# Chunked cross-attention with instance norm: the mask's negatives laid in the score banks by the scalar engine

## The reference

```python
qh, kh, vh = proj(ctx, W_in, b_in)            # (tokens, 256) @ (256, 768), 8 heads of 32
scores = einsum('bnqhd,bnkhd->bnhqk', qh, kh) / sqrt(32)     # inside each chunk of 64
scores = scores + where(mask > 0, 0.0, -1e9)                 # by key
out = einsum('bnhqk,bnkhd->bnqhd', softmax(scores), vh)
out = (out @ W_out.T + b_out) * mask + x
return (out - mean(out, tokens)) * rsqrt(var(out, tokens) + 1e-5)
```

## Time and profile before

| what | value |
|---|---|
| median of 3 runs | 2059.18 us (2058.57 to 2062.14) |
| the profiled execution's own time | 2053.5 us |
| its span, first to last instruction | 2051.7 us |
| mean granted clock of TensorE | 0.991 of full speed |
| busy: PE / DVE / ACT / POOL | 97% / 82% / 72% / 76% |

### The profile page before, as it was taken

How to read it: one execution, slowest core, us unless ns; L and a number is a source line. 1 busy time by engine, 2 the same in 40 slices (tenths; PEclk the granted TensorE clock), 3 DMA queues, 4 the chain that set the end, 5 groups by cost and what they waited for, 6 DMA issues and landing times.

```text
span 2051.7 us, 95454 instructions
## 1 busy us (share of the span) xinstructions
PE 1999.4 (97%) x42504; PEld 1633.8 (80%) x42504; DVE 1682.0 (82%) x2053; ACT 1487.3 (72%) x2177; POOL 1560.4 (76%) x1062
## 2 busy tenths in 40 slices
PE   6999999999999999999999999999999999999994
PEld 5888888888888888888888888888788887887883
DVE  4788888888888888888888888888888887888884
ACT  4677777777777777777777777777777777776774
POOL 4777777787777777777778787777777777877773
PEclk9999999999999999999999999999999999999996
DMA  4456666556656556656555665556665556655554
GB/s 155 116 151 175 171 180 182 166 155 176 180 170 171 173 165 177 182 172 169 161 168 172 188 180 161 158 172 177 172 176 168 161 171 173 179 164 154 163 152 129
DMA packets 242904, 342.81 MB, mean 167 GB/s; under 512 B 28992, under 2 KB 94784, under 8 KB 242496
## 3 DMA queue, kind: packets, MB, share of 16 engines
q1 hardware_dynamic: 242496, 336.71, 57.0%
HBM read 168.82 MB, written 67.11 MB: 115 GB/s over the span
## 4 chain that ended last, share of the span: by engine, by line
PE 96%; issue 1%; POOL 1%; ACT 1%; DVE 0%; DMA 0%; SPq 0%; POOLq 0%; ACTq 0%; DVEq 0%
PE proj_bank L291 37%; PE proj_bank L323 19%; PE proj_bank L345 18%; PE o_bank L392 10%; PE score_bank L368 9%; PE score_bank L361 3%; POOL y L554 0%; DMA ctx_raw<-ctx 0%; POOL ctx_lo L544 0%; ACT y L495 0%; POOL neg_rows L567 0%; ACT ctx_hi L427 0%; POOL prob L537 0%; POOL o_lo L576 0%; ACT q_f L466 0%
## 5 line engine op out<-in xcount | busy, mean ns | idle before, releaser
L537 POOL TENSOR_TENSOR prob<-prob,recip 128x1024 f32<-128x1024 f32 x256 | 487.8, 1905 | 329.4 <-DVE recip L627 327.2
L612 DVE TENSOR_REDUCE row_max<-score_bank 128x16 f32<-128x1024 f32 x256 | 313.4, 1224 | 298.9 <-PE score_bank L368 297.9
L435 ACT ACTIVATE prob<-prob 128x1024 f32<-128x1024 f32 x256 | 271.5, 1060 | 283.1 <-DVE prob L616 283.1
L544 POOL TENSOR_TENSOR ctx_lo<-ctx_raw,ctx_hi 128x512 fp32r<-128x512 f32 x256 | 331.0, 1293 | 48.8 <-ACT ctx_hi L427 48.5
L291 PE MATMUL proj_bank<-ctx_hi,w_hi 128*128 128x512 f32 x1024 | 349.0, 422 | 5.7 <-POOL ctx_lo L544 4.3
L554 POOL TENSOR_TENSOR y<-y,x_raw 128x512 f32<-128x512 f32 x256 | 325.4, 1293 | 4.6 <-DVE y L655 4.6
L616 DVE TENSOR_TENSOR prob<-score_bank,row_max 128x1024 f32<-128x1024 f32 x256 | 313.4, 1224 | 8.8
L291 PE MATMUL proj_bank<-ctx_hi,w_lo 128*128 128x512 f32 x1024 | 320.6, 394 | 0.0
L291 PE MATMUL proj_bank<-ctx_lo,w_hi 128*128 128x512 f32 x1024 | 318.0, 392 | 0.0
L635 DVE STREAM_TRANSPOSE squares<-prob 128x1024 f32<-128x1024 f32 x256 | 315.8, 1234 | 2.0 <-POOL prob L537 2.0
L623 DVE TENSOR_REDUCE sums<-prob 128x16 f32<-128x1024 f32 x256 | 304.7, 1190 | 1.2 <-ACT prob L435 1.1
(11 more groups left out here) (44 smaller groups left out, 3781.9 us busy)
## 6 DMA issues: line engine op xcount, KB each, us to landing
ctx_raw<-ctx SPq DMA_DIRECT2D x128, 512.0 KB, 5.8
x_raw<-x SPq DMA_DIRECT2D x128, 512.0 KB, 4.6
prob_t<-squares SPq DMA_DIRECT2D x1024, 64.0 KB, 2.5
out<-y SPq DMA_DIRECT2D x128, 512.0 KB, 6.0
mask_all<-mask SPq DMA_DIRECT2D x128, 256.0 KB, 4.2
v_x<-v_f SPq DMA_DIRECT2D x256, 128.0 KB, 3.5
y<-w_in_t SPq DMA_DIRECT2D x1, 768.0 KB, 4.4
y<-w_out_t SPq DMA_DIRECT2D x1, 256.0 KB, 4.4
```

The lines of the kernel that those rows point to most:

```text
L537: pool.tensor_tensor(part, part, slots(recip[:, u % 2, :]), ALU.mult).then_inc(norm_done, 1)
L544: pool.tensor_tensor(ctx_lo[:, n % 2, :, tokens], ctx_raw[:, n % BLOCKS, :, tokens], ctx_hi[:, n % 2, :, tokens].bitcast(F32), ALU.subtrac ...
L612: dve.tensor_reduce(row_max[:, :].rearrange("p (r c) -> p r c", c=CPU), rows, AX_X, ALU.max).then_inc(max_done, 1)
```

## The change

The eight mask matmuls of each unit go. In their place the scalar engine copies the negatives, now in fp32, into the four score banks (`lay_negatives`), a unit ahead, behind `high_attention`; the scores wait for that copy (`seeded`) and accumulate on it. Eight matmuls of zeros at the start (`open_banks`) put the banks in the state in which matmuls add. The copy of the attention output into `o_f` goes, and VectorE makes the low part of attention for both units, straight from `o_bank`. GpSimd loses its `low_attention` and gains the second half of the normalise, ahead of `divide`; the scalar engine keeps the first half.

```diff
@@ tensor, scores
-                wait(pe, less_done, count(B, UNITS, u))
-                for r in range(ROWS):
-                    masked = neg_rows[r * DH:r * DH + 1, j % 2, h * UNIT:(h + 1) * UNIT]
-                    for f in range(HALVES):
-                        pe.matmul(score_bank[f * CHUNK:(f + 1) * CHUNK, r, 0:UNIT], ones_row[r * DH:r * DH + 1, :],
-                                  masked, start=True, stop=False, skip_group_check=True)
+                pe.wait_ge(seeded, count(B, UNITS, u + 1))
...
+            def open_banks():
+                for r in range(ROWS):
+                    head = slice(r * DH, (r + 1) * DH)
+                    for f in range(HALVES):
+                        last = pe.matmul(score_bank[f * CHUNK:(f + 1) * CHUNK, r, 0:UNIT], zero_rows[head, 0:CHUNK],
+                                         zero_rows[head, :], start=True, stop=True, skip_group_check=True)
+                last.then_inc(opened, 1)
@@ tensor, probs_times_v
-                if h == 0:
-                    wait(pe, o_lo_done[1], n)
-                else:
-                    pe.wait_ge(o_f_done, n + 1)
+                wait(pe, o_lo_done, UPB * n + h)
@@ scalar
+            def lay_negatives(B, u):
+                if not unit_there(B, u):
+                    return
+                j, h = u // UPB, u % UPB
+                if h == 0:
+                    act.wait_ge(neg_done, count(B, BLOCKS, j + 1))
+                if B == 0 and u == 0:
+                    act.wait_ge(opened, 1)
+                wait(act, less_done, count(B, UNITS, u))
+                act.activation(score_bank[:, :, 0:UNIT], neg_rows[:, j % 2, h * UNIT:(h + 1) * UNIT].unsqueeze(
+                    1).broadcast_to([P, ROWS, UNIT]), ACT.Copy).then_inc(seeded, 1)
...
-                    normalise(done, 0)
+                    normalise(done)
...
                     high_attention(B, u - 2)
-                    if h == 0:
-                        copy_attention(B, u - 2)
-                    normalise(done, 1)
+                    lay_negatives(B, u + 2)
                     copy_squares(B, u)
@@ gpsimd
+            def normalise(n):
+                if not block_there(0, n):
+                    return
+                batch, j = n // BLOCKS, n % BLOCKS
+                if j == 0:
+                    pool.wait_ge(shift_done, batch + 1)
+                part = y[:, batch % 2, 1, j, :]
+                pool.tensor_scalar(part, part, rstd[:, 1:2], shift[:, 1:2], ALU.mult, ALU.add).then_inc(z_done[1], 1)
...
                         masked_keys(B, j + 1)
-                        low_attention(B, u - 2)
                     else:
...
+                    normalise(BLOCKS * (B - 1) + u - 5 if u >= 5 else BLOCKS * (B - 2) + 3 if u == 0 else -1)
                     divide(B, u + 1)
@@ vector
-                dve.tensor_tensor(o_lo[:, m % 2, 1, :, :], o_units, o_hi[:, m % 2, 1, :, :].bitcast(F32),
-                                  ALU.subtract).then_inc(o_lo_done[1], 1)
+                dve.tensor_tensor(o_lo[:, m % 2, h, :, :], o_units, o_hi[:, m % 2, h, :, :].bitcast(F32),
+                                  ALU.subtract).then_inc(o_lo_done, 1)
...
-                    if h == 1:
-                        low_attention(B, u - 2)
+                    low_attention(B, u - 2)
@@ buffers and the store
-        neg_rows = sb("neg_rows", [P, 2, BLOCK], BF16)
+        neg_rows = sb("neg_rows", [P, 2, BLOCK], F32)
-                sp.wait_ge(z_done, 2 * n + 2)
+                for f in range(HALVES):
+                    sp.wait_ge(z_done[f], n + 1)
```

More of the change, by code:

```diff
@@ L66, in attention_kernel @@
         b_final = sb("b_final", [P, HALVES], F32)
-        ones_row = sb("ones_row", [P, CHUNK], BF16)
+        zero_rows = sb("zero_rows", [P, UNIT], F32)
         minus_half = sb("minus_half", [P, HALVES], F32)
@@ L85, in attention_kernel @@
         o_lo = sb("o_lo", [P, 2, UPB, HALVES, UNIT], F32R)
-        o_f = sb("o_f", [P, HALVES, UNIT], F32)
         stats = sb("stats", [P, HALVES, BLOCKS, 6], F32)
@@ L126, in attention_kernel @@
         rows_done = sem("rows_done")
+        seeded = sem("seeded")
+        opened = sem("opened")
         max_done = sem("max_done")
@@ L137, in attention_kernel @@
         o_hi_done = sem("o_hi_done")
-        o_f_done = sem("o_f_done")
-        o_lo_done = [sem("o_lo_done0"), sem("o_lo_done1")]
+        o_lo_done = sem("o_lo_done")
         y_done = sem("y_done")
@@ L146, in attention_kernel @@
         shift_done = sem("shift_done")
-        z_done = sem("z_done")
+        z_done = [sem("z_done0"), sem("z_done1")]
         block = stack.enter_context(nc.Block())
@@ L341, in project_out @@
                     if f == 0 and a == 2:
-                        for h in range(UPB):
-                            pe.wait_ge(o_lo_done[h], count(B, BLOCKS, m + 1))
+                        pe.wait_ge(o_lo_done, count(B, UNITS, UPB * (m + 1)))
                     for h in range(HALVES):
@@ L369, in scores @@
                                              q_f[head, j % 2, f, tokens], k_f[head, j % 2, f, tokens], start=False,
[L370 removed]
+                                             stop=True, skip_group_check=True)
                 last.then_inc(rows_done, 1)
+            def open_banks():
[5 more added lines that the diff above has]
+                last.then_inc(opened, 1)
             def probs_times_v(B, u):
@@ L398, in _ @@
             pe.wait_ge(pool_const, 2)
+            open_banks()
             def steps(B):
@@ L444, in high_attention @@
                 act.activation(o_hi[:, m % 2, h, :, :], o_units, ACT.Copy).then_inc(o_hi_done, 1)
[L446 to L451, removed]
             def copy_squares(B, u):
@@ L484, in values @@
                                proj_bank[:, h, :], ACT.Copy).then_inc(v_f_done, 1)
-            def normalise(n, f):
+            def normalise(n):
                 if not block_there(0, n):
@@ L490, in normalise @@
                 batch, j = n // BLOCKS, n % BLOCKS
-                if j == 0 and f == 0:
+                if j == 0:
                     act.wait_ge(rstd_done, batch + 1)
                     act.wait_ge(shift_done, batch + 1)
-                part = y[:, batch % 2, f, j, :]
-                act.activation(part, part, ACT.Identity, bias=shift[:, f:f + 1],
-                               scale=rstd[:, f:f + 1]).then_inc(z_done, 1)
+                part = y[:, batch % 2, 0, j, :]
+                act.activation(part, part, ACT.Identity, bias=shift[:, 0:1],
+                               scale=rstd[:, 0:1]).then_inc(z_done[0], 1)
             def steps(B):
@@ L528, in _ @@
             pool.memset(minus_half[:, :], -0.5).then_inc(pool_const, 1)
-            pool.memset(ones_row[:, :], 1.0).then_inc(pool_const, 1)
+            pool.memset(zero_rows[:, :], 0.0).then_inc(pool_const, 1)
             pool.wait_ge(pool_const, 2)
@@ L568, in masked_keys, with normalise @@
                                    ALU.mult).then_inc(neg_done, 1)
-            def low_attention(B, u):
-                if not unit_there(B, u):
+            def normalise(n):
+                if not block_there(0, n):
                     return
[L574 to L577, removed]
+                batch, j = n // BLOCKS, n % BLOCKS
+                if j == 0:
+                    pool.wait_ge(shift_done, batch + 1)
+                part = y[:, batch % 2, 1, j, :]
+                pool.tensor_scalar(part, part, rstd[:, 1:2], shift[:, 1:2], ALU.mult, ALU.add).then_inc(z_done[1], 1)
             def steps(B):
```

4 lines of the change are left out of this document (1 added, 3 removed).

## The result

The changed kernel takes 2039.92 us (median of 4, 2037.81 to 2047.37) against 2058.88 beside it: a ratio of 0.9916, 95% interval 0.9892 to 0.994. That is 19 us less where 27 were forecast. The profiled execution took 2037.81, its span is 2036.0 us, 15.7 less than before.

What follows compares the result with a forecast made beforehand. TensorE's own sequence was taken as the bound (busy 97%, 96% of the chain). Mask -33, weight load up to +8, tail +2, middle -27: 2032 against a median of 2059.2; range 2013 to 2058, the forecast case 2013 to 2044 (chance 0.66).

Steps and rivals of the forecast that it cites:

- its own signs of being wrong: Scores waiting for the laying, or key projection for values, by tenths of a microsecond a step; scores' block over 0.88 us.
- Part 1: TensorE: 2048 mask matmuls go, 0.13 us a step by starts, 33 us off; bounds 20 and 51.
- an open weight load: TensorE: first scores' weight load, 130 ns against the mask's 101, may lie exposed: 8 us back.
- The rival that took the chain's 0.25 us: TensorE: mask matmuls cost 0.25 us a step, so 64 us off, 1995; chance 0.04.
- Part 2: Scalar engine: laying the negatives takes 1.06 us per unit, covered by 0.4 us at the two tightest places, costed at nothing.
- Part 3: VectorE: 128 more low-attention subtractions of 629 ns, 80 us, in even steps; covered, some 0.7 us of waiting a step remains.
- Part 4: GpSimd: loses 128 subtractions (167 us), gains 128 normalises at 1.93 us, net +80 us; fits; fp32 negatives taken at 1.93.
- The tail: End of kernel: eight normalises, 5.74 us on the scalar engine, become four there and four on GpSimd, 7.7: +2 us.
- The sum: Whole kernel: -31 with the first weight load covered, -23 with it open; middle taken, -27 us, giving 2032.
- The slower rival: GpSimd's negatives come late through laying, copy_squares, values, key projection; slack 0.43 us; at 2.9 us about 2100; chance 0.14.
- no change: Laying at 1.18 and negatives at 2.3 make the path 0.5 longer, eating most of the gain: 2055 to 2063; chance 0.08.
- a part is given back: Stalls of about 0.1 us in the tight steps: 2044 to 2055 us; chance 0.08.

Runs made afterwards that it cites:

- the second measurement: The changed kernel as it is, run again beside the version with two queue exchanges: 2045.44 us, ratio 0.9954 to the kernel before.

## Why the prediction came out as it did

- **What bounds it: right, and the reason for the sign.** TensorE's own sequence set the end, and taking work out of it shortened the end. But the chain is TensorE's for 71%, where the prediction had about 96%, and one of its own signs of being wrong is there: the key projection waits for the values, by 0.2 us, in one step of eight.
- **Part 1, the mask's price: right.** 0.13 us a step by starts; 0.125 measured, 32 us. The 8 us set aside for an open weight load do not show. The rival that took the chain's 0.25 us fell with the run without the mask.
- **Part 2, the laying "costed at nothing": the step that failed.** Its length was right (1.06 forecast, 1.03 measured), and so was the path, but the slack of 0.4 us was read in one pair of steps (those of rows 7 and 8), where the reciprocal standard deviation does not occur. In step 4 it stands ahead of the negatives, and VectorE's closing of the batch's statistics makes the division late before that; there the slack was used up, and TensorE lost 0.22 x 32 = 7 us. Moving 0.71 us out of that path took the wait away.
- **Part 3, low attention: a term missing.** Its time was right (628 ns), and VectorE's wait for scores fell to 168.6 us, 0.66 a step, where 0.7 was forecast. But I priced the instruction and not what stands behind it in its queue. In step 4 that is the shift, which before fell between GpSimd's low attention and its division, and now falls into the division: 0.24 x 32 = 8 us. The Trainium skill (SBUF — State Buffer, section "Who interferes with whom") says that a VectorE instruction with two SBUF inputs contends with a GpSimd instruction that reads SBUF, and that the second to start blocks until the first ends. Behind the division the trace agrees (1.5 us, ending with it); during the negatives, which read SBUF too, it does not (0.15 us). The order agrees as well: with the negatives computed twice, the shift took 1.85 us or more in the 14 batches in which it started 0.02 to 0.07 us behind the division, and 0.16 us in those in which it started ahead of it or within 0.01 us.
- **Part 4, GpSimd: mis-sized.** The normalise took 0.78 us, not 1.93: the row I took as nearest shares the instruction's kind, not its operations (a comparison and a product there, a product and a sum here). GpSimd's busy time fell by 64 us where +80 was forecast. That 1.93 would have been covered as well, as I had it, no run shows. The estimate of 0.43 us that I made in the prediction from the Trainium skill (GPSIMD Engine Reference, section 4.1, Engine selection) is nearer to the 0.78 than mine was; for the negatives, 1.93, it is far off.
- **The tail.** Forecast +2 us; the eight normalises that took 5.74 us now take 3.03 in two halves side by side (GpSimd's: 2027.80 to 2030.83), so -2.7. With 0.78 us for the normalise in place of 1.93 the forecast's own sum would have had this sign.
- **The sum.** Forecast -33, up to +8, +2. The 15.7 us between the two profiled spans fall in three stretches: 0.2 up to the 25th unit's scores, 11.7 from there to the second-last unit's, and 3.7 behind them. In the middle stretch, 28.75 batches, the medians give -29 for the mask and +15 for what the steps lost again (61.49 against 60.97), and stalls +2.4 (16.3 against 13.9): -11.6. That the time lies in the range is partly luck: two waits of 15 us that were not in the sum, against a tail and a weight load that together came out some 9 us better. On the second measurement, 11 us, the time is 2045, in the range but no longer in the forecast's 2013 to 2044.
- **The slower rival: right as a mechanism,** with its place, and at its price within a third (1.93 us more would be 192 us by its slack of 0.43; it was 140); in the changed kernel it decided in one step of eight. What I said of *no change* and of *a part is given back*, that a part of the gain would be eaten in tight steps, is nearer to what took place than the reason I gave for the forecast. The price of *no change* was wrong by its own terms: a path 0.5 us longer over a slack of 0.43 loses 0.07 x 128 = 9 us, which leaves 2041 and not 2055 to 2063.

The forecast took the relief of the scalar engine as two small subtractions in its sum. The runs with the laying alone (38 us slower than before, some 30 of them by the steps) and with both halves of the normalise on it (46 us lost) show that they decide the sign.

## What to carry to other kernels

When slack is read for a new chain, read it in the worst step of the longest period, not in a typical one: what happens once per batch (here 0.71 us of GpSimd and a 128x2 shift) stands in the same queues. When an instruction is added, look at what moves behind it: the cheap one that lands beside another engine's long instruction can cost more than the one added. An engine that is 80% busy over the span can still be late in half of the steps, as the scalar engine was with both halves of the normalise on it.

## What the runs showed of the hardware

- A 128x2 VectorE instruction with two SBUF tensor inputs took 1.54 us when it started inside GpSimd's division (two tensor inputs) and ended with it; 0.10 us when GpSimd was idle; 0.15 us inside a GpSimd instruction with one tensor input; 0.16 us where it started before the division did. With one tensor input and a per-partition scalar, two 128x1 instructions inside the division took 0.20 us each.
- Two GpSimd tensor_scalar instructions of 128x512 elements took 1927 ns (comparison, product; 1925 with bf16 output) and 778 ns (product, sum with per-partition scalars).
- TensorE loses 7 to 26 us an execution, in every version run here, in stalls of 0.2 to 4.4 us that the profile puts to no engine. They differ from run to run and blur comparisons of a few us; medians of steps mostly do not have them (they do behind unit 3 with the laying alone). 152 of 153 such idle stretches over 0.15 us end 2.2 to 2.7 us after the start of a 16 KB packet that loads instructions.
